# State-space stage of a decoder layer on one core: the sums over states as plain products with a standing identity, by channels, two steps behind the scan

## The chip, the cores and the metric

The kernel runs on one core of a Trainium2 chip. The metric is the device time of one execution in microseconds (us), the median of the runs shown. TensorE is called PE, VectorE DVE, ScalarE ACT, GpSimd POOL, and SyncE, which issues the transfers, SP.

## The reference, cut to what matters

A decoder layer on x of shape (16, 256, 512): a state-space block, then cross-attention, then a feed-forward block. Only the first is touched:

```python
B, L, H, DI, N, R, K = (1, 256, 512, 1024, 16, 128, 4)   # b is 16 here
hs = einsum('blh,dh->bdl', x, W_in_states); gate = einsum('blh,dh->bdl', x, W_in_gates)
hs = silu(conv(hs, conv_w) + conv_b)                     # 4 taps along l
dt = softplus((hst @ W_dt.T) @ W_dtproj.T + b_dtproj)
Bm, Cm = hst @ W_b.T, hst @ W_c.T                        # (b, l, 16)
s[l] = exp(A * dt[l]) * s[l-1] + dt[l] * Bm[l] * hs[l]   # for 1024 channels x 16 states
y[d, l] = sum_n s[l][d, n] * Cm[l, n]
y = (y + hs * D) * silu(gate)
out = einsum('bdl,od->blo', y, W_out)
```

All of it is in float32.

## The kernel before, in words

The state-space stage works through 16 batches. The 1024 channels are 8 tiles of 128 partitions, the 16 states of a tile are 4 groups of 4, and so a batch has 32 steps: step k is tile k // 4, group k % 4, four states of 256 positions. In a step

- ACT makes the decays `exp(A dt)` into PSUM, in two halves (`decays`, L708: 4 activations of 256). It waits until the bank of two steps before is free: for the product with C of step k-2, or for its scan where POOL takes the product.
- POOL makes the inputs `dt B u` (`inputs`, L830), up to four steps ahead.
- DVE runs the recurrence, in two halves (`scan`, L914). In 22 of the steps DVE also multiplies the states by C into `hc` (`times_C`, L926), two buffers that are used in turn; in the other 10, `POOL_STEPS`, the scan writes `hp` and POOL multiplies (L839), three steps behind.
- PE adds the four states and collects them over the four steps of the tile in one PSUM bank, `y_ps` (`sum_states`, L526). Each 128x128 piece of `hc` or `hp` is the stationary operand and the identity the moving one, with `is_transpose`, accumulating: the sum comes out turned, positions on the partitions, 8 products of 128 columns in a step. The skip term `u * D` starts each tile (`skip_term`, L511: 2 products with `diagD`, 128 columns each). DVE steps are summed in the step itself, POOL steps two steps later (`SUM_AT`).
- After a tile's last sum DVE multiplies by the gate (`finish_y`, L937) into `yT`. The skip term of the next tile waits for it (`y_ready`), since `y_ps` is one bank.

Besides, PE works through the products for the batches around it, called units: "s" input projection, "c" convolution (with diagonal matrices), "g" gate (made with positions on the partitions), "l" the projections to B, C and the low-rank dt, "d" dt of two tiles, "t" the turning back of two tiles of `yT` to channels, and "o" the output projection. `PRODUCTS` says how many products a unit has and `PER` how many units of the kind a batch has. `plan` deals them out over the 32 steps, so that each step has the same cost by `COST`; the order of the long ones is `LONG`, and short ones start at the steps in `SHORT`. Each unit goes to one of 3 PSUM banks in turn, and first waits until the unit three before has been taken out of its bank. ACT takes a unit out `LAG` steps after the step in which it ended (`evacuate`; DVE does so for "o", `add_residual`, L949), behind its own decays of that step.

PE's order in a step: units, then the skip term in every fourth step, then the sum. DVE's: scan, residual, product with C, and in every fourth step `finish_y`. Engines wait for each other by counting semaphores alone; the order on each engine is as written. The last batch has no "s", "c", "g", "l" for a next one, and its "o" is dealt out by `LAST_OUT`.

Of the kernel before, what the change touches and what calls it, by code (L numbers as in the profile page):

```python
# [48 lines left out]
SHORT = [(0, "d", 1, 0), (3, "t", 3, -1), (6, "d", 2, 0), (11, "t", 0, 0), (12, "d", 3, 0), (18, "t", 1, 0),  # L49
         (23, "d", 0, 1), (26, "t", 2, 0)]  # L50
# [12 lines left out]
LAG = {"s": 2, "c": 2, "g": 2, "l": 3, "d": 2, "t": 2, "o": 1}  # L63
SKIP_COST = 0.5
# [22 lines left out]
BU_OF = [(k % BUS,) for k in range(STEPS)]  # L87


def user_before(k, buffer, of):  # L90

    return next((i for i in range(k - 1, k - STEPS - 1, -1) if buffer in of[i % STEPS]))


def plan():
# [3 lines left out]
    rate = (work + DT * SKIP_COST) / STEPS  # L99

    def room(k):
        return rate * (k + 1) - (k // CPT + 1) * SKIP_COST

# [33 lines left out]
FINISH_LATE = True  # L137
# [5 lines left out]
def state_space_phase(nc, xT, x, w_in, w_bc, w_dt, w_dtproj, w_out, chan, ident, w_ffn, bc_scratch, w_scales, x1,  # L143
                      ctxt, mask, wq, wk, chan_qk, stack_d, mask_d, x1n_d):
# [5 lines left out]
    with ExitStack() as ctx:  # L150
# [28 lines left out]
        gate = sb("gate", [P, 2, SEQT, INNER])  # L179
        du = sb("du", [P, 2 * GRP, SEQ])  # L180
        y = sb("y", [P, 2, DT, SEQ])
        yT = sb("yT", [P, 2, SEQT, P])
        bc = sb("bc", [P, CPT, 2, CHUNK])
# [22 lines left out]
        mk_rows = bu[0:BATCH, 0:3].rearrange("b i c -> b (i c)").bitcast(BF16).rearrange("b (o r t) -> b o r t", o=2, r=len(PAIRS))  # L206
# [5 lines left out]
        y_ps = ps("y_ps", [P, 4, P])  # L212
# [21 lines left out]
        b_in = [sem(f"b_in{i}") for i in range(CPT)]  # L234
# [97 lines left out]

        def pool_products(b, k):

            return b * len(POOL_STEPS) + sum(i <= k for i in POOL_STEPS)
# [13 lines left out]
        def _(sp):  # L349
# [19 lines left out]
            def spread(c, side, arrived):  # L369
# [3 lines left out]
                sp.dma_start(bc[:, c, side, :], src).then_inc(arrived[c], 16)  # L373
# [21 lines left out]
            for c in range(CPT):  # L395
                spread(c, 0, b_in)
                spread(c, 1, c_in)
# [20 lines left out]
            for b in range(BATCH):  # L418
# [8 lines left out]
                if active(f):  # L427
                    for c in range(CPT):
                        sp.wait_ge(bu_done, (b + 1) * STEPS - CPT + c + 1)
                        spread(c, 0, b_in)  # L430
# [4 lines left out]
                if active(f):  # L435
                    if b == BATCH - 2:
                        load_first_rows()
                    for c in range(CPT):
                        sp.wait_ge(hc_pool, pool_products(b, max(k for k in POOL_STEPS if k % CPT == c or k == 0)))
                        sp.wait_ge(hc_dve, half_product(b, max(k for k in DVE_STEPS if k % CPT == c), HALVES - 1))  # L440
                        spread(c, 1, c_in)
# [19 lines left out]
        def _(pe):  # L461
            pe.wait_ge(params, 2 * 16)

            def unit(bank, kind, i, f, par, lo, hi):

                n, proj = PRODUCTS[kind], proj_banks[:, bank]
                if kind == "o" and is_last(f):
                    pe.wait_ge(ev["t"], seq("t", f, (hi - 1) // GRP))
                elif lo == 0:
# [8 lines left out]
                    if kind == "t":  # L478
                        pe.wait_ge(y_ready, f * DT + GRP * i + GRP)
                    if kind == "o" and i == 0:  # L480
                        pe.wait_ge(ev["t"], (f + 1) * GROUPS)
                for k in range(lo, hi):
# [3 lines left out]
                    elif kind == "g":  # L486
                        m = pe.matmul(proj[:, :], xT_sb[:, k, i % 2 * P:(i % 2 + 1) * P],  # L487
                                      win_sb[:, k, 1, i // 2 * HID:(i // 2 + 1) * HID], start=start, stop=stop)
# [10 lines left out]
                    elif kind == "t":  # L499
                        m = pe.transpose(proj[:, k * P:(k + 1) * P], yT[:, k // SEQT, k % SEQT, :], id_sb[:, :])  # L500
# [125 lines left out]
            def tail():  # L626
                pe.wait_ge(w_added, BATCH)
# [8 lines left out]
                pe.wait_ge(ev["t"], seq("t", b, GROUPS - 2))  # L636
                unit(0, "t", GROUPS - 1, b, 1, 0, PRODUCTS["t"])
# [6 lines left out]
        def _(act):  # L644
# [13 lines left out]
            def evacuate(bank, kind, i, f, par):  # L658
# [12 lines left out]
                elif kind == "g":  # L671
                    act.activation(gate[:, par, i % 2, i // 2 * HID:(i // 2 + 1) * HID], proj[:, :], ACT.Copy).then_inc(ev["g"], 1)
# [22 lines left out]
            def decays(b, k):  # L695
# [3 lines left out]
                b0, k0 = (b, k - BACK) if k >= BACK else (b - 1, k - BACK + STEPS)  # L699
                for half in range(HALVES):  # L700
                    if not (isinstance(b, int) and b == 0 and k < BACK):
                        if k0 in POOL_STEPS:
                            act.wait_ge(scan_done, half_of(b0, k0, half))
                        else:
                            act.wait_ge(hc_dve, half_product(b0, k0, half))
                    for i in range(NS // HALVES):
                        n, bank, first = half * NS // HALVES + i, bank_of_half(k, half), i * SEQ
                        a = act.activation(states[:, bank, first:first + SEQ], dt[:, t, :], ACT.Exp,  # L708
                                           scale=negA[:, t, c * NS + n:c * NS + n + 1])
# [83 lines left out]
            def tail():  # L793
                evacuate(0, "t", GROUPS - 1, BATCH - 1, 1)

            over_batches(act, front, body, tail)

        @block.gpsimd
        def _(pool):
# [20 lines left out]
            def inputs(b, k):  # L820
# [5 lines left out]
                buf, = BU_OF[k]  # L826
                before = user_before(k, buf, BU_OF)
                if not (isinstance(b, int) and b == 0 and before < 0):
                    pool.wait_ge(scan_done, half_of(b, before, HALVES - 1))
                pool.tensor_tensor(bu[:, buf, :].rearrange("p (n l) -> p n l", n=NS),  # L830
                                   du[:, t % (2 * GRP):t % (2 * GRP) + 1, :].to_broadcast([P, NS, SEQ]),
                                   bc[:, c, 0, :].rearrange("p (n l) -> p n l", n=NS), ALU.mult).then_inc(bu_done, 1)

            def times_C(b, k):
# [4 lines left out]
                pool.tensor_tensor(h, h, bc[:, k % CPT, 1, :], ALU.mult).then_inc(hc_pool, 1)  # L839
# [32 lines left out]
        def _(dve):  # L872
# [32 lines left out]
            def scan(b, k):  # L905
# [4 lines left out]
                for half in range(HALVES):  # L910
# [3 lines left out]
                    dve.tensor_tensor_scan(dst, src, bu[:, BU_OF[k][0], cols], 0.0, ALU.mult, ALU.add).then_inc(scan_done, 1)  # L914

            def times_C(b, k):
# [4 lines left out]
                for half in range(HALVES):  # L921
# [4 lines left out]
                    dve.tensor_tensor(hc[:, i % 2, cols], states[:, bank_of_half(k, half), :], bc[:, c, 1, cols], ALU.mult)\  # L926
                       .then_inc(hc_dve, 1)

            def finish_y(b, par, t):
# [30 lines left out]
            def body(b, par):  # L960
                for k in range(STEPS):
                    scan(b, k)
                    for (kind, i), (_, at) in ROWS_AT.items():
                        if is_last(b) and at == k:
                            first_rows(kind, i)
                    if not FINISH_LATE:
                        finish(b, par, k)
# [5 lines left out]
                    if FINISH_LATE:  # L973
                        finish(b, par, k)
# [1012 lines left out]
def build(nc, ins, out):  # L1987

    def dram(name, shape, dt=F32):
# [10 lines left out]
                      ins["chan"], ins["ident"], ins["w_ffn"], dram("bc_scratch", (2 * STATES, SEQ)), w_scales, x1,  # L2000
# [49 lines left out]
```

## Time and profile before

| | |
|---|---|
| median of 3 runs | 3173.97 us (3173.22 to 3177.13) |
| span of the profiled execution | 3175.0 us |
| PE busy | 2991.9 us (94%) |
| PE weight load busy | 1833.1 us (58%) |
| DVE busy | 2833.2 us (89%) |
| ACT busy | 2419.9 us (76%) |
| POOL busy | 2094.4 us (66%) |
| granted clock of PE, mean | 0.977 |

The state-space stage is the first 1750 us of the span. Busy time counts any moment in which an instruction of the engine is recorded as running. On PE an instruction's record is longer than the time until the next one may start, so the capacity that is used up is read from the distance between starts in a run of equal products.

### The profile page before, as it was taken

Reading aid. Unit: us, or ns where it says so; the run is one execution under the profiler, and the core shown is the slowest. Engines: PE = TensorE matmul, PEld = TensorE weight load, DVE = VectorE, ACT = ScalarE, POOL = GpSimd, SP = SyncE. Lnnn points to the kernel's source line nnn. Section 1 sums busy time; section 2 is a strip of 40 time slices with the busy share of each in tenths; the row PEclk is TensorE's granted clock in tenths of the full one; section 3 lists DMA queues with packets and bytes.
Section 4 is the critical chain, followed back from the end, with each engine's and each line's share of the span. In section 5 each row is a group of like instructions: output and inputs, shape, how many; then the busy total and the mean of one; then the engine's idle time right before and its main releaser. Section 6 shows DMA issues by size and latency. Waiting matters only on the chain. (4 is left out here: it accounts for less than half of the span.)

```text
span 3175.0 us, 47891 instructions
## 1 busy us (share of the span) xinstructions
PE 2991.9 (94%) x16134; PEld 1833.1 (58%) x16134; DVE 2833.2 (89%) x4149; ACT 2419.9 (76%) x4531; POOL 2094.4 (66%) x1207
## 2 busy tenths in 40 slices
PE   7899999999999999999987699999999999799998
PEld 4777677767776777777755244444444444244444
DVE  6999999999999999999998788888888888288887
ACT  4888888888888888888875177777777777577786
POOL 5999999999999999999998234334334334100000
PEclk9999999999999999999998699999999999899999
DMA  4112211222022202220221656655655653221111
GB/s 176 32 46 81 81 49 43 80 81 69 23 80 81 79 13 80 84 81 15 77 96 64 180 163 178 182 181 174 186 181 171 183 180 113 101 77 47 47 41 37
DMA packets 164389, 311.97 MB, mean 98 GB/s; under 512 B 22736, under 2 KB 80208, under 8 KB 164000
## 3 DMA queue, kind: packets, MB, share of 16 engines
q1 hardware_dynamic: 158784, 299.53, 29.6%
q10 hardware_dynamic: 5360, 9.38, 1.0%
q8 instruction: 129, 2.11, 0.3%
q14 instruction: 116, 0.95, 0.1%
HBM read 217.16 MB, written 91.69 MB: 97 GB/s over the span
## 5 line engine op out<-in xcount | busy, mean ns | idle before, releaser
L830 POOL TENSOR_TENSOR bu<-du,bc 128x1024 f32<-128x1024 f32 x512 | 1199.0, 2370 | 32.1 <-DMA bc<-bc_scratch 29.9
L708 ACT ACTIVATE states<-dt,negA 128x256 f32<-128x256 f32 x2048 | 852.8, 463 | 240.2 <-DVE hc L926 229.4
L914 DVE TENSOR_TENSOR_SCAN states<-states,bu 128x512 f32<-128x512 f32 x704 | 821.5, 1212 | 10.5 <-ACT states L708 8.2
L1568 DVE TENSOR_REDUCE mmax<-s_ps 128x1 f32<-128x512 f32 x1024 | 673.0, 686 | 126.1 <-PE s_ps L1288 105.2
L1413 ACT ACTIVATE pt<-s_ps 128x512 f32<-128x512 f32 x1024 | 579.6, 595 | 209.5 <-PE s_ps L1297 203.7
L926 DVE TENSOR_TENSOR hc<-states,bc 128x512 f32<-128x512 f32 x704 | 445.7, 674 | 1.6 <-DMA bc<-bc_scratch 1.6
L1288 PE MATMUL s_ps<-kst,qst 102*128 102x512 bf16 x1024 | 400.5, 393 | 28.6 <-DMA kst<-mask_d 19.3
L526 PEld LDWEIGHTS y_ps<-id_sb,hc 128*128 128x128 f32 x2816 | 330.7, 143 | 122.9 <-DVE hc L926 58.2
L526 PE MATMUL y_ps<-id_sb,hc 128*128 128x128 f32 x2816 | 377.1, 277 | 22.8 <-DVE hc L926 22.8
L1297 PE MATMUL s_ps<-qst,kst 105*128 105x512 bf16 x1024 | 387.4, 382 | 5.8 <-ACT pt L1413 3.9
L839 POOL TENSOR_TENSOR hp<-hp,bc 128x1024 f32<-128x1024 f32 x160 | 379.5, 2372 | 2.8 <-DVE hp L914 1.9
L914 DVE TENSOR_TENSOR_SCAN hp<-states,bu 128x512 f32<-128x512 f32 x320 | 372.2, 1204 | 5.2 <-ACT states L708 5.2
L1308 PE MATMUL pv_ps<-pt,vaug 128*32 128x512 f32 x2048 | 272.1, 604 | 1.6 <-ACT pt L1413 1.2
L1288 PEld LDWEIGHTS s_ps<-kst,qst 102*128 102x128 bf16 x1024 | 100.0, 98 | 298.6 <-DVE mmax L1568 187.3
L490 PE MATMUL proj<-xpad,diagW 128*128 128x256 f32 x960 | 245.1, 385 | 27.6 <-ACT xpad L667 27.6
L485 PE MATMUL proj<-xT_sb,win_sb 128*128 128x256 f32 x1024 | 252.8, 384 | 16.0 <-DMA win_sb<-in_w_in 7.2
L487 PE MATMUL proj<-win_sb,xT_sb 128*128 128x512 f32 x512 | 243.0, 594 | 0.0
L1817 PE MATMUL gu_ps<-gu,xqT 128*128 128x512 bf16 x1024 | 234.9, 383 | 8.0 <-ACT xqT L1870 6.3
L502 PE MATMUL proj<-wout_sb,y 128*128 128x512 f32 x512 | 240.8, 600 | 1.3 <-ACT y L679 1.3
L490 PEld LDWEIGHTS proj<-xpad,diagW 128*128 128x128 f32 x960 | 173.7, 191 | 67.8 <-issue 49.1
L485 PEld LDWEIGHTS proj<-xT_sb,win_sb 128*128 128x128 f32 x1024 | 189.1, 193 | 39.0 <-issue 10.7
L526 PE MATMUL y_ps<-id_sb,hp 128*128 128x128 f32 x1280 | 171.6, 278 | 8.2 <-POOL hp L839 7.4
(172 smaller groups left out, 4170.6 us busy)
## 6 DMA issues: line engine op xcount, KB each, us to landing
bc<-bc_scratch SPq DMA_DIRECT2D x128, 512.0 KB, 5.2
stack_d<-parts SPq DMA_DIRECT2D x180, 256.0 KB, 3.0
qst<-stack_d SPq DMA_DIRECT2D x64, 384.0 KB
kst<-stack_d SPq DMA_DIRECT2D x64, 384.0 KB
x<-xres SPq DMA_DIRECT2D x31, 512.0 KB, 4.8
w_raw<-in_w_ffn SPq DMA_DIRECT2D x48, 256.0 KB, 2.8
w_raw<-in_w_ffn SPq DMA_DIRECT2D x16, 768.0 KB, 7.3
xT_sb<-in_xT SPq DMA_DIRECT2D x16, 512.0 KB, 6.0
```

The source lines that it names most:

```text
L485: m = pe.matmul(proj[:, 0:SEQ], win_sb[:, k, 0, i * P:(i + 1) * P], xT_sb[:, k, :], start=start, stop=stop)
L490: m = pe.matmul(proj[:, 0:SEQ], diagW[:, i, k, :], xpad[:, i % 2, k:k + SEQ], start=start, stop=stop)
L526: m = pe.matmul(y_ps[:, i, :], src[:, n * SEQ + i * P:n * SEQ + (i + 1) * P], id_sb[:, :], start=False, stop=(c == CPT - 1 and n == NS - 1 ...
L708: a = act.activation(states[:, bank, first:first + SEQ], dt[:, t, :], ACT.Exp, scale=negA[:, t, c * NS + n:c * NS + n + 1])
L830: pool.tensor_tensor(bu[:, buf, :].rearrange("p (n l) -> p n l", n=NS), du[:, t % (2 * GRP):t % (2 * GRP) + 1, :].to_broadcast([P, NS, SEQ ...
L839: pool.tensor_tensor(h, h, bc[:, k % CPT, 1, :], ALU.mult).then_inc(hc_pool, 1)
L914: dve.tensor_tensor_scan(dst, src, bu[:, BU_OF[k][0], cols], 0.0, ALU.mult, ALU.add).then_inc(scan_done, 1)
L926: dve.tensor_tensor(hc[:, i % 2, cols], states[:, bank_of_half(k, half), :], bc[:, c, 1, cols], ALU.mult)\
L1288: pe.matmul(s1_ps[:, n % S_BANKS, :], qst[0:ROWS1, par, u, tt * P:(tt + 1) * P], kst[0:ROWS1, par, u, :], start=True, stop=True).then_inc( ...
L1297: pe.matmul(s2_ps[:, n % S_BANKS, :], kst[0:ROWS2, par, u, st * P:(st + 1) * P], qst[0:ROWS2, par, u, :], start=True, stop=True).then_inc( ...
L1413: act.activation(pt[:, g % 2, u % HG, st, :], s2_ps[:, score(b, u, st) % S_BANKS], ACT.Exp).then_inc(exp_done, 1)
L1568: dve.tensor_reduce(mmax[:, u // HG, c:c + 1], s1_ps[:, n % S_BANKS], AX.X, ALU.max).then_inc(s1_free, 1)
```

## The change

The sums are turned round: the identity is the stationary operand and the states are the moving one, in a plain product of 256 columns, so that the sum has channels on the partitions. The gate is made in that layout too, `finish_y` writes `y` directly, and the "t" units with their evacuations go. The sums of all steps, and the skip term with them, are made two steps later. `finish_y` moves to DVE's step k with (k - 2) % 4 == 0, ahead of the product with C. The plan drops "t", counts a skip term as 1 and a gate unit as 8 products of 256 columns; the order in `LONG` stays. Other edits rename (`bc` to `bcB` and `bcC`, `BU_OF` to `k % BUS`) or move the mask rows' scratch from `bu` to `y`.

```diff
-PRODUCTS = {"s": HK, "c": TAPS, "g": HK, "l": 2 * DT, "d": GRP, "t": GRP * SEQT, "o": DT}
-COST = {"s": 1, "c": 1, "g": 2, "l": 1, "d": 1, "t": 0.25, "o": 2}
-PER = {"s": DT, "c": DT, "g": 4, "l": 1, "d": GROUPS, "t": GROUPS, "o": SEQT}
+PRODUCTS = {"s": HK, "c": TAPS, "g": GRP * HK, "l": 2 * DT, "d": GRP, "o": DT}
+COST = {"s": 1, "c": 1, "g": 1, "l": 1, "d": 1, "o": 2}
+PER = {"s": DT, "c": DT, "g": GROUPS, "l": 1, "d": GROUPS, "o": SEQT}
...
-SHORT = [(0, "d", 1, 0), (3, "t", 3, -1), (6, "d", 2, 0), (11, "t", 0, 0), (12, "d", 3, 0), (18, "t", 1, 0),
-         (23, "d", 0, 1), (26, "t", 2, 0)]
+SHORT = [(0, "d", 1, 0), (6, "d", 2, 0), (12, "d", 3, 0), (23, "d", 0, 1)]
...
                     elif kind == "g":
-                        m = pe.matmul(proj[:, :], xT_sb[:, k, i % 2 * P:(i % 2 + 1) * P],
-                                      win_sb[:, k, 1, i // 2 * HID:(i // 2 + 1) * HID], start=start, stop=stop)
+                        t, h = GRP * i + k // HK, k % HK
+                        m = pe.matmul(proj[:, k // HK * SEQ:(k // HK + 1) * SEQ], win_sb[:, h, 1, t * P:(t + 1) * P],
+                                      xT_sb[:, h, :], start=(h == 0), stop=(h == HK - 1))
...
-                    elif kind == "t":
-                        m = pe.transpose(proj[:, k * P:(k + 1) * P], yT[:, k // SEQT, k % SEQT, :], id_sb[:, :])
...
             def skip_term(b, par, t):
 
-                if not (isinstance(b, int) and b == 0 and t == 0):
+                if b * DT + t > 0:
                     pe.wait_ge(y_ready, b * DT + t)
-                for i in range(SEQT):
-                    pe.matmul(y_ps[:, i, :], u[:, par, t, i * P:(i + 1) * P], diagD[:, t, :],
-                              start=(i == 0), stop=False, skip_group_check=True)
+                pe.matmul(y_ps[:, :], diagD[:, t, :], u[:, par, t, :], start=True, stop=False, skip_group_check=True)
...
-                    for i in range(SEQT):
-                        m = pe.matmul(y_ps[:, i, :], src[:, n * SEQ + i * P:n * SEQ + (i + 1) * P], id_sb[:, :],
-                                      start=False, stop=(c == CPT - 1 and n == NS - 1), is_transpose=True,
-                                      skip_group_check=True)
+                    m = pe.matmul(y_ps[:, :], id_sb[:, :], src[:, n * SEQ:(n + 1) * SEQ],
+                                  start=False, stop=(c == CPT - 1 and n == NS - 1), skip_group_check=True)
...
+            def tile_sums(b, par, k):
+
+                if k % CPT == 0:
+                    skip_term(b, par, k // CPT)
+                sum_states(b, k)
...
                 for k in range(STEPS):
-                    if k % CPT == 0 and k - SUM_AT in POOL_STEPS:
-                        sum_states(b, k - SUM_AT)
...
-                    if k % CPT == 0:
-                        skip_term(b, par, k // CPT)
-                    if k not in POOL_STEPS:
-                        sum_states(b, k)
-                    if k % CPT and k - SUM_AT in POOL_STEPS:
-                        sum_states(b, k - SUM_AT)
+                    if k >= SUM_AT:
+                        tile_sums(b, par, k - SUM_AT)
+                    elif b > 0:
+                        tile_sums(b - 1, 1 - par, k - SUM_AT + STEPS)
...
-                elif kind == "t":
-                    act.activation(y[:, par, GRP * i:GRP * i + GRP, :].rearrange("p t l -> p (t l)"), proj[:, :], ACT.Copy)\
-                       .then_inc(ev["t"], 1)
...
-                if not (isinstance(b, int) and b == 0 and t < 2):
-                    dve.wait_ge(mm["t"], b * GROUPS + (t - 2) // GRP + 1)
-                dve.tensor_tensor(yT[:, t % 2], gate[:, par, :, t * P:(t + 1) * P], y_ps[:, 0:SEQT, :], ALU.mult).then_inc(y_ready, 1)
+                if t == 0 and b > 1:
+                    dve.wait_ge(mm["o"], (b - 1) * PER["o"])
+                dve.tensor_tensor(y[:, par, t, :], gate[:, par, t, :], y_ps[:, :], ALU.mult).then_inc(y_ready, 1)
 
             def finish(b, par, k):
-                if k == 0 and active(b - 1):
-                    finish_y(b - 1, 1 - par, DT - 1)
-                elif k and k % CPT == 0:
-                    finish_y(b, par, k // CPT - 1)
+
+                t = (k - SUM_AT) // CPT - 1
+                if (k - SUM_AT) % CPT == 0 and t >= 0:
+                    finish_y(b, par, t)
+                elif (k - SUM_AT) % CPT == 0 and active(b - 1):
+                    finish_y(b - 1, 1 - par, t + DT)
```

## Rows read from the trace of the kernel before

**Rows 1.** The page's first part, and two rows of its 40 slices.
```profile
PE 2991.9 (94%) x16134; PEld 1833.1 (58%) x16134; DVE 2833.2 (89%) x4149; ACT 2419.9 (76%) x4531; POOL 2094.4 (66%) x1207
...
PE   7899999999999999999987699999999999799998
...
PEclk9999999999999999999998699999999999899999
```

**Rows 2.** Stretches: length, busy time and instructions by engine, clock, DMA share, GB/s.
```profile
310.00:800.00 490.00, 473.85 (x2548) 355.75 (x2547) 481.27 (x559) 413.49 (x858) 484.83 (x240) 1.00 0.20 68
```

**Rows 3.** ACT's evacuation of "l", once a batch, in order of time.
```profile
134.92 0.36 ACT L676 ACTIVATE bc_sb<-proj 32x256 f32<-32x256 f32 x1
240.41 0.36 ACT L676 ACTIVATE bc_sb<-proj 32x256 f32<-32x256 f32 x1
...
1594.65 0.36 ACT L676 ACTIVATE bc_sb<-proj 32x256 f32<-32x256 f32 x1
```

**Rows 4.** Groups by line and shape, 800 to 1012 us.
```profile
L830 POOL TENSOR_TENSOR bu<-du,bc 128x1024 f32<-128x1024 f32 x66 | 154.8, 2381 | 0.0
L708 ACT ACTIVATE states<-dt,negA 128x256 f32<-128x256 f32 x262 | 109.1, 463 | 29.2 <-DVE hc L926 28.4 <-DVE hp L914 0.5
...
L526 PE MATMUL y_ps<-id_sb,hc 128*128 128x128 f32 x360 | 46.9, 273 | 0.0
...
L490 PE MATMUL proj<-xpad,diagW 128*128 128x256 f32 x134 | 33.8, 382 | 3.2 <-ACT xpad L667 3.2
...
L526 PE MATMUL y_ps<-id_sb,hp 128*128 128x128 f32 x168 | 22.0, 274 | 0.1
...
L682 ACT ACT_TABLE_LOAD x8 | 10.3, 1283 | 1.9 <-PE proj L497 1.8
...
L511 PE MATMUL y_ps<-diagD,u 128*128 128x128 f32 x64 | 9.7, 274 | 0.0
...
L497 PE MATMUL proj<-dtlow,wdtp_sb 128*128 128x256 f32 x32 | 8.4, 386 | 3.5 <-DVE xres L949 3.5
...
L685 ACT ACTIVATE dt<-proj,chan_sb 128x256 f32<-128x256 f32 x16 | 6.7, 471 | 0.1
L937 DVE TENSOR_TENSOR yT<-gate,y_ps 128x256 f32<-128x256 f32 x16 | 6.6, 411 | 4.4 <-PE y_ps L526 3.2 <-issue 0.9
...
L667 ACT ACTIVATE xpad<-proj 128x256 f32<-128x256 f32 x16 | 5.7, 369 | 1.1 <-PE proj L485 1.0
...
L679 ACT ACTIVATE y<-proj 128x512 f32<-128x512 f32 x8 | 4.6, 581 | 0.1
...
L500 PE MATMUL proj<-id_sb,yT 128*128 128x128 f32 x32 | 4.8, 272 | 0.0
```

**Rows 5.** Matmuls in order of time, runs of equal ones merged: start, length, count.
```profile
768.83 4.46 PE L502 MATMUL proj<-wout_sb,y 128*128 128x512 f32 x10
...
821.23 0.61 PE L511 MATMUL y_ps<-diagD,u 128*128 128x128 f32 x4
821.67 1.04 PE L526 MATMUL y_ps<-id_sb,hc 128*128 128x128 f32 x8
...
822.98 1.89 PE L485 MATMUL proj<-xT_sb,win_sb 128*128 128x256 f32 x8
...
827.09 1.70 PEld L490 LDWEIGHTS proj<-xpad,diagW 128*128 128x128 f32 x8
```

**Rows 6.** DVE in order of time, around 822 us.
```profile
822.26 1.26 DVE L926 TENSOR_TENSOR hc<-states,bc 128x512 f32<-128x512 f32 x2
...
823.45 2.32 DVE L914 TENSOR_TENSOR_SCAN hp<-states,bu 128x512 f32<-128x512 f32 x2
...
825.69 2.32 DVE L914 TENSOR_TENSOR_SCAN states<-states,bu 128x512 f32<-128x512 f32 x2
```

**Rows 7.** PE in order of time, in the last batch.
```profile
1721.27 1.97 PE L526 MATMUL y_ps<-id_sb,hc 128*128 128x128 f32 x8 [2.13 <-DVE hc L926]
```

**Rows 8.** L526 alone, whole run: what PE idled for ahead of it, us and times.
```profile
  DVE hc L926: 81.0, 130
```

More of the change, by code:

```diff
@@ L86, with fixed @@
 POOL_AT, SUM_AT = 3, 2
-BU_OF = [(k % BUS,) for k in range(STEPS)]
-def user_before(k, buffer, of):
-    return next((i for i in range(k - 1, k - STEPS - 1, -1) if buffer in of[i % STEPS]))
+SKIP_COST = 1
+def fixed(k):
+    return sum(SKIP_COST * ((i - SUM_AT) % CPT == 0) for i in range(k + 1))
 def plan():
@@ L98, in plan @@
     work = sum(PRODUCTS[kind] * COST[kind] for kind, _, _ in LONG) + sum(PRODUCTS[k] * COST[k] for _, k, _, _ in SHORT)
-    rate = (work + DT * SKIP_COST) / STEPS
+    rate = (work + fixed(STEPS - 1)) / STEPS
     def room(k):
-        return rate * (k + 1) - (k // CPT + 1) * SKIP_COST
+        return rate * (k + 1) - fixed(k)
     step, spent = 0, 0
@@ L140, with state_space_phase @@
     assert GRP * CPT * (_j - 1) - 1 <= _at < GRP * CPT * _j, (_j, _at)
-def state_space_phase(nc, xT, x, w_in, w_bc, w_dt, w_dtproj, w_out, chan, ident, w_ffn, bc_scratch, w_scales, x1,
-                      ctxt, mask, wq, wk, chan_qk, stack_d, mask_d, x1n_d):
+def state_space_phase(nc, xT, x, w_in, w_bc, w_dt, w_dtproj, w_out, chan, ident, w_ffn, bc_scratch, w_scales,
+                      x1, ctxt, mask, wq, wk, chan_qk, stack_d, mask_d, x1n_d):
     with ExitStack() as ctx:
@@ L178, in state_space_phase @@
         dt = sb("dt", [P, DT, SEQ])
-        gate = sb("gate", [P, 2, SEQT, INNER])
+        gate = sb("gate", [P, 2, DT, SEQ])
         du = sb("du", [P, 2 * GRP, SEQ])
         y = sb("y", [P, 2, DT, SEQ])
-        yT = sb("yT", [P, 2, SEQT, P])
-        bc = sb("bc", [P, CPT, 2, CHUNK])
+        bcB = sb("bcB", [P, CPT, CHUNK])
+        bcC = sb("bcC", [P, CPT, CHUNK])
         bu = sb("bu", [P, BUS, CHUNK])
@@ L233, in state_space_phase @@
         xres_in = sem("xres_in")
-        b_in = [sem(f"b_in{i}") for i in range(CPT)]
+        b_in = [sem(f"b_in{c}") for c in range(CPT)]
         c_in = [sem(f"c_in{i}") for i in range(CPT)]
@@ L331, in products, with bank_before @@
             return b * len(DVE_STEPS) + sum(i <= k for i in DVE_STEPS)
+        def bank_before(b, k):
+            n = b * STEPS + k - BACK
+            return None if n < 0 else (n // STEPS, n % STEPS)
         def pool_products(b, k):
@@ L367, in load_piece, with spread, spread_B, spread_C @@
                 sp.dma_start(w_raw[:, :], src[:, i * PART:(i + 1) * PART]).then_inc(w_piece_in, 16)
-            def spread(c, side, arrived):
+            def spread(c, side, dst, arrived):
                 first = (2 * c + side) * NS
                 src = bc_scratch[first:first + NS, :].rearrange("n l -> (n l)").partition_broadcast(P)
-                sp.dma_start(bc[:, c, side, :], src).then_inc(arrived[c], 16)
+                sp.dma_start(dst, src).then_inc(arrived, 16)
+            def spread_B(c):
+                spread(c, 0, bcB[:, c, :], b_in[c])
+            def spread_C(c):
+                spread(c, 1, bcC[:, c, :], c_in[c])
             def save_bc(f):
@@ L395, in _ @@
             for c in range(CPT):
-                spread(c, 0, b_in)
-                spread(c, 1, c_in)
+                spread_B(c)
+                spread_C(c)
             sp.wait_ge(mm["g"], PER["g"])
@@ L618, in body @@
                             unit(pos % PROJ, kind, i, b + off, par if off == 0 else 1 - par, lo, hi)
-                    if k % CPT == 0:
-                        skip_term(b, par, k // CPT)
-                    if k not in POOL_STEPS:
-                        sum_states(b, k)
-                    if k % CPT and k - SUM_AT in POOL_STEPS:
-                        sum_states(b, k - SUM_AT)
+                    if k >= SUM_AT:
+                        tile_sums(b, par, k - SUM_AT)
+                    elif b > 0:
+                        tile_sums(b - 1, 1 - par, k - SUM_AT + STEPS)
             def tail():
+                for k in range(STEPS - SUM_AT, STEPS):
+                    tile_sums(BATCH - 1, 1, k)
                 pe.wait_ge(w_added, BATCH)
@@ L671, in evacuate @@
                 elif kind == "g":
-                    act.activation(gate[:, par, i % 2, i // 2 * HID:(i // 2 + 1) * HID], proj[:, :], ACT.Copy).then_inc(ev["g"], 1)
+                    act.activation(gate[:, par, GRP * i:GRP * i + GRP, :].rearrange("p t l -> p (t l)"), proj[:, :], ACT.Copy)\
+                       .then_inc(ev["g"], 1)
                 elif kind == "l":
@@ L698, in decays @@
                     act.wait_ge(du_ready, b * GROUPS + t // GRP + 1)
-                b0, k0 = (b, k - BACK) if k >= BACK else (b - 1, k - BACK + STEPS)
+                before = bank_before(b, k)
                 for half in range(HALVES):
[L701 to L705, printed above, removed]
+                    if before is not None and before[1] in POOL_STEPS:
+                        act.wait_ge(scan_done, half_of(*before, half))
+                    elif before is not None:
+                        act.wait_ge(hc_dve, half_product(*before, half))
                     for i in range(NS // HALVES):
-                        n, bank, first = half * NS // HALVES + i, bank_of_half(k, half), i * SEQ
-                        a = act.activation(states[:, bank, first:first + SEQ], dt[:, t, :], ACT.Exp,
-                                           scale=negA[:, t, c * NS + n:c * NS + n + 1])
+                        n = half * NS // HALVES + i
+                        dst = states[:, bank_of_half(k, half), i * SEQ:(i + 1) * SEQ]
+                        a = act.activation(dst, dt[:, t, :], ACT.Exp, scale=negA[:, t, c * NS + n:c * NS + n + 1])
                     a.then_inc(decay_ready, 1)
@@ L825, in inputs @@
                     pool.wait_ge(du_ready, b * GROUPS + t // GRP + 1)
[L826 to L829, printed above, removed]
+                buf = k % BUS
+                if b * STEPS + k >= BUS:
+                    pool.wait_ge(scan_done, half_of(b, k - BUS, HALVES - 1))
                 pool.tensor_tensor(bu[:, buf, :].rearrange("p (n l) -> p n l", n=NS),
                                    du[:, t % (2 * GRP):t % (2 * GRP) + 1, :].to_broadcast([P, NS, SEQ]),
-                                   bc[:, c, 0, :].rearrange("p (n l) -> p n l", n=NS), ALU.mult).then_inc(bu_done, 1)
+                                   bcB[:, c, :].rearrange("p (n l) -> p n l", n=NS), ALU.mult).then_inc(bu_done, 1)
             def times_C(b, k):
@@ L925, in times_C @@
                     dve.wait_ge(scan_done, half_of(b, k, half))
-                    dve.tensor_tensor(hc[:, i % 2, cols], states[:, bank_of_half(k, half), :], bc[:, c, 1, cols], ALU.mult)\
+                    dve.tensor_tensor(hc[:, i % 2, cols], states[:, bank_of_half(k, half), :], bcC[:, c, cols], ALU.mult)\
                        .then_inc(hc_dve, 1)
@@ L962, in body @@
                     scan(b, k)
+                    finish(b, par, k)
                     for (kind, i), (_, at) in ROWS_AT.items():
@@ L972, in body @@
                         times_C(b, k)
-                    if FINISH_LATE:
-                        finish(b, par, k)
             def tail():
```

33 lines of the change are left out of this document (12 added, 21 removed).

## Prediction

> **What bounds the kernel now.** I began with the page's busy shares and its 40 slices [rows 1]. PE is at 9 tenths or more through nearly all of the stage that the change touches, at full clock. The stretch from 310 to 800 us [rows 2] has PE busy for 473.85 of 490 us, DVE 481.27 and POOL 484.83, ACT only 413.49. So three engines look full at once. PE's figure alone says little, because its records overlap; what counts is the distance between starts.
>
> The length of a batch comes from an instruction that runs once in it [rows 3]: from 240.41 to 1594.65 us are 13 batches, (1594.65 - 240.41) / 13 = 104.2 us. The first interval, 134.92 to 240.41, is 105.5 us although batch 0 has no "o" units; the period there is set by DVE and POOL. DVE's own work: a scan pair occupies 2.24 us (825.69 - 823.45) and a pair of products with C 1.19 us (823.45 - 822.26) [rows 6]; 32 x 2.24 + 22 x 1.19 = 97.9 us, plus eight `finish_y` at about 0.35 and two residuals at about 0.6, 101.9 us.
>
> PE's work in a batch. The distance between starts is (length of a run - one instruction) / (count - 1) [rows 4, 5]: for 256 columns (1.89 - 0.385) / 7 = 0.215 us; for 512, (4.46 - 0.60) / 9 = 0.429; for a turning sum of 128, (1.04 - 0.273) / 7 = 0.110; for the skip term, 128 plain columns, (0.61 - 0.274) / 3 = 0.112. The weight load of a 256-column product is no bound: eight take 1.70 us beside 1.89 us of products.
>
> The row to see is how many instructions a product becomes [rows 4]. The two batches of that view have 2 x 4 x 4 = 32 "t" products, and L500 has x32: one each. The sums have 8 products a step, and 360 + 168 = 528 = 66 x 8 for the 66 steps that POOL's x66 counts: one each. The skip term has 2 x 8 x 2 = 32 products and L511 has x64: **two instructions each**. "d" has 2 x 4 x 2 = 16 products and L497 x32: two each. So a plain float32 product is issued twice, and one with `is_transpose` once. Per batch, in instructions: "s" 64, "c" 64, "l" 32, "d" 16 at 0.215 = 37.8 us; "g" 32 and "o" 32 at 0.429 = 27.5; sums 256 at 0.110 = 28.2; skip 32 at 0.112 = 3.6; "t" 16 at 0.110 = 1.8. Together **98.9 us of 104.2**: PE is 95% used up, and has 5.3 us of room.
>
> **The change, part by part.**
>
> *Sums.* A step had 8 turning products, 8 x 0.110 = 0.88 us. It gets 4 plain ones of 256 columns = 8 instructions at 0.215 = 1.72 us. That the identity stands still saves nothing, as the loads lie beside the products. 32 x (1.72 - 0.88) = **+26.9 us a batch**. Bounds: the product isn't in this trace, but "s" and "c" have its shape, type, accumulation and operand memories, so 0.215 is firm; below, if it were one instruction, 0.86 a step and the term -0.6.
>
> *Skip term.* 4 x 0.112 becomes 2 x 0.215: 8 x -0.02 = -0.1 us. *"t" units.* 16 instructions go: -1.8 us on PE; on ACT 4 x 0.58 = -2.3 us [rows 4], on an engine with room, worth nothing. *Gate.* 32 x 0.429 = 13.7 becomes 64 x 0.215 = 13.8 us: nothing. *`finish_y`* has the same 128x256 shape and stays at 0.41 us. Transfers are the same in number and size; the renamed buffers cost nothing, and the mask rows' scratch serves only the start.
>
> PE's work is then 98.9 + 26.9 - 0.1 - 1.8 = **123.9 us a batch**, above DVE's 101.9: PE alone sets the period.
>
> The Trainium skill bears on this in two places. Perfetto Trace Analysis, section Transposes, says to do transposes in the transpose mode rather than by a standard matmul, as they skip arithmetic; the change gives up such products for plain ones. TensorE: Matmul & The Clock Gate, section Terms, calls the mode four times faster for FP32. In this trace [rows 4, 5] it is 2 x 0.112 against 0.110 us for 128 columns, a factor of 2. By the page a plain product would cost 0.44 us, the sums 32 x 8 x 0.33 = +84 us a batch; the trace disagrees, and the rows' term stands.
>
> *Two steps behind.* The sums waited 81.0 us for `hc` over the whole run [rows 8], at most 5 us a batch, and less in the middle (no idle time ahead of their matmuls in rows 4). This wait goes; with PE the bound it is already outside the 123.9. New waits matter more. Call E(k) the end of PE's step k; a step has about 5 cost units of 0.43 us and a sum of 1.72, 3.87 us. The product with C needs its `hc` buffer back, so the third of three DVE steps in a row (k = 3, 9, 13, 19, 31) can't end before E(k) + 0.63. Steps 10 and 14 follow such a step and finish a tile: E + 0.63, scan 2.32, `finish_y` 0.41 = E + 3.4. Behind that stands PE's skip term, and all of PE's queue behind it; the plan by the new costs gives these steps 4 units, so PE is there at E + 1.72. Each loses about **1.7 us**. The other six finishes follow a step whose buffer was freed a step or more earlier: the scan is done by E + 1.3, covered by the units.
>
> *First convolution.* c0 stands first in step 2 and needs s0 out of its bank, which ACT does in its step 3. From E(31): product 0.63, scan 2.24, half the decays of step 2 0.83, then the softplus of d1 with its two table loads 1.28 + 0.94 + 1.28, decays 1.67, copy 0.37 = 9.2 us [rows 4, 6]. PE arrives after 10 units and two sums, 4.3 + 3.4 = 7.7. **1.5 us** lost; the corresponding waits now are L490's 3.2 us in two batches [rows 4]. The wait of "d" for the residual, 3.5 us in two batches, falls away: d1 now takes the bank of o0, which ended in step 26, and o1's bank goes to s1, a step later.
>
> Sum: 123.9 + 1.7 + 1.7 + 1.5 + about 1 for semaphore gaps (now 104.2 - 98.9 - 3.4 = 1.9 are unnamed) = **129.8 us, +25.6 a batch**. Bounds: no stall at all, 123.9 (+19.7); a stall of 1.7 at all eight tiles and 3 us at c0 gives about 141, against which the other six covers speak; I take 135 as the upper one.
>
> *Ends.* Batch 0 has no "o" (13.8 us less) and no sums in its first two steps (3.4 less): 23 steps at 3.88 - 3.4 + 4 of waits = 90, then 9 steps at DVE's 3.26 = 29, 119 against 105.5 with a start that is unchanged: about +12 us. The last batch has only "d" and "o", so DVE sets it; its sums there run at the lower clock level, 0.22 a piece [rows 7] ((1.97 - 0.4) / 7), and even doubled they take 3.5 us, about a DVE step. Two sums trail at the end and the "t" units with their copy are gone from it: +3.
>
> Profile's own time 3175 + 12 + 14 x 25.6 + 3 = **3548 us**. The span is within 0.1% of the median of the runs shown, 3173.97, so I don't rescale. The later stages aren't touched.
>
> **Rivals.**
> *PE bound, waits as worked out* (3500 to 3600): speaks for it that both the count and the distance are read from shapes in the same kernel. Chance 0.72.
> *PE bound, waits hidden*: if DVE and ACT run far enough ahead, 124 to 126 us: 3175 + 6 + 14 x 20.7 = 3470. 0.11.
> *PE bound, waits multiply*: evacuations hold ACT, ACT holds decays, these `finish_y`, all tiles stall; 135 us and more: 3175 + 15 + 14 x 31 = 3624 upward. 0.12.
> *The other side: the sum isn't issued twice.* If a product with the standing identity were one instruction of 0.215, PE's work would be 96.4 us, DVE and POOL would set the period at 102 to 104, and with the waits on "d" and for `hc` gone the time 3175 - 16 x 1.5 = 3150. It decides from the point where the sum step costs under 1.1 us (PE under 104). Every plain product of this kernel speaks against it. 0.03; 0.02 for no change.
>
> The range holds the three PE cases up to a period of 135: 3450 to 3620. What a measurement can tell from no change is about 0.2%. Slower by more 0.95, within 0.02, faster 0.03.
>
> **What would show it.** L526's group should have the same count, x4096 in all, with 128x256 shapes and runs of 8 in 1.89 us; L676 every 130 us; DVE and POOL busy about 80% of the stage; PE waiting at the skip term for `finish_y` twice a batch near steps 10 and 14, and at the first L490. A sum group of x2048 would mean the last rival. A DVE that is never idle would mean that I misread its room.

## The result, and the profile after

The changed kernel takes 3573.19 us (3569.74 to 3575.2), the one before 3175.38 us beside it: a ratio of **1.1254, 95% interval 1.1238 to 1.127**. The forecast was 3548 us in a range of 3450 to 3620, slower with a chance of 0.95.

The page's first part and two of its slice rows (its span is cut in 40 equal slices, a digit is the busy share in tenths), as [rows 1] for the kernel before:

```profile
PE 3369.1 (94%) x16101; PEld 2230.3 (62%) x16134; DVE 2858.7 (80%) x4149; ACT 2404.0 (67%) x4467; POOL 2095.8 (59%) x1207
...
DVE  6778778778777778777877887888888888648887
...
PEclk9999999999999999999999997999999999989999
```

DVE and POOL are busy for about as long as before (2833.2 and 2094.4 us) in a span that is 398 us longer, and DVE's slices of the stage fall from 9 to 7 and 8. Its row on the page of the kernel before:

```profile
DVE  6999999999999999999998788888888888288887
```

PE's share is 94% in both pages, so the share says nothing; PE's busy time grew by 377 us.

The same stretch as in [rows 2]:

```profile
310.00:800.00 490.00, 470.34 (x2052) 381.95 (x2051) 387.70 (x442) 321.82 (x667) 381.82 (x189) 1.00 0.14 47
```

POOL makes 189 instructions in it instead of 240: the same 490 us hold 3.75 batches (of 130.57 us, worked out below) where they held 4.70. That is why PE's busy column hardly moves (470 against 474). For one batch it is 470.34 / 3.75 = 125.3 us against 473.85 / 4.70 = 100.7, so PE's work a batch grew by about 25 us, and the batch with it.

The identity stands still, but every product still has its own weight load. From the page's groups:

```profile
L528 PE MATMUL y_ps<-hc,id_sb 128*128 128x256 f32 x2816 | 669.4, 381 | 0.0
L528 PEld LDWEIGHTS y_ps<-hc,id_sb 128*128 128x128 f32 x2816 | 538.7, 191 | 105.6 <-issue 34.9
```

The once-in-a-batch instruction (the evacuation of "l"), as [rows 3], in order of time:

```profile
155.17 0.36 ACT L680 ACTIVATE bc_sb<-proj 32x256 f32<-32x256 f32 x1
280.25 0.36 ACT L680 ACTIVATE bc_sb<-proj 32x256 f32<-32x256 f32 x1
...
1977.64 0.36 ACT L680 ACTIVATE bc_sb<-proj 32x256 f32<-32x256 f32 x1
```

The period is (1977.64 - 280.25) / 13 = **130.57 us**, where it was 104.17. Up to ACT's step 24 of batch 1, where this instruction stands, the kernel is 280.25 - 240.41 = 39.8 us late, the 13 periods add 343.2, and the last stretch of the stage, to the first instruction of the attention stage on DVE (2151.32 us, before 1751.41), adds 173.68 - 156.76 = 16.9. The stages behind give 1.5 back; together that is the 398 us.

The groups of instructions from 800 to 1064 us, as [rows 4], two batches:

```profile
L528 PE MATMUL y_ps<-hc,id_sb 128*128 128x256 f32 x355 | 84.0, 379 | 0.0
...
L922 DVE TENSOR_TENSOR hc<-states,bcC 128x512 f32<-128x512 f32 x88 | 58.0, 683 | 40.3 <-PE y_ps L528 39.4
...
L497 PE MATMUL proj<-xpad,diagW 128*128 128x256 f32 x128 | 31.7, 380 | 3.4 <-ACT xpad L670 3.4
...
L515 PE MATMUL y_ps<-u,diagD 128*128 128x256 f32 x34 | 10.7, 397 | 6.5 <-DVE y L933 6.5
```

```profile
L926 DVE TENSOR_TENSOR hc<-states,bc 128x512 f32<-128x512 f32 x90 | 56.9, 673 | 0.0
```

The last row is of the kernel before, 800 to 1012 us. DVE now waits 39.4 us for PE to free `hc`, where it waited for nothing. PE waits in two places only: 6.5 us in two batches at the skip term, 3.4 at the first convolution (`c` of tile 0).

PE in order of time around step 14 of a batch, then DVE in the same stretch:

```profile
895.72 1.89 PE L528 MATMUL y_ps<-hc,id_sb 128*128 128x256 f32 x8
897.45 1.46 PE L491 MATMUL proj<-xT_sb,win_sb 128*128 128x256 f32 x6
898.74 0.59 PE L497 MATMUL proj<-xpad,diagW 128*128 128x256 f32 x2
900.95 0.70 PE L515 MATMUL y_ps<-u,diagD 128*128 128x256 f32 x2 [1.61 <-DVE y L933]
```

```profile
896.78 0.69 DVE L922 TENSOR_TENSOR hc<-states,bcC 128x512 f32<-128x512 f32 x1 [3.97 <-PE y_ps L528]
897.65 0.69 DVE L922 TENSOR_TENSOR hc<-states,bcC 128x512 f32<-128x512 f32 x1 [0.17 <-PE y_ps L528]
898.25 2.33 DVE L910 TENSOR_TENSOR_SCAN hp<-states,bu 128x512 f32<-128x512 f32 x2
900.50 0.40 DVE L933 TENSOR_TENSOR y<-gate,y_ps 128x256 f32<-128x256 f32 x1
```

Read from the top: 8 sum instructions from 895.72, the next product starts at 897.45, that is 1.73 us for a step's sum. As PE ends the sum, DVE may fill the buffer (897.65), then scans, then finishes the tile at 900.90, and the skip term starts 0.05 us later. The row gives 1.61 us of idle time, counted from the end of the last record. By distances PE loses more: without the wait the skip term would have started at 898.74 + 2 x 0.215 = 899.17, so 1.78 us are lost, and its second instruction comes 0.32 us behind the first (0.70 - 0.38) in place of 0.215. That makes 1.88. The wait at the first convolution, in the same way:

```profile
975.85 1.89 PE L528 MATMUL y_ps<-hc,id_sb 128*128 128x256 f32 x8
979.43 1.97 PE L497 MATMUL proj<-xpad,diagW 128*128 128x256 f32 x8 [1.69 <-ACT xpad L670]
```

It would have started at 975.85 + 8 x 0.215 = 977.57, and its eight instructions take (1.97 - 0.38) - 7 x 0.215 = 0.08 us more than their distances: 1.94 us in all.

### The profile page after: what moved, and what is told of

Its sections match the earlier page's. It is cut to its first block and busy times, and to the rows that moved or that the text cites. A ratio compares the mean times of both kernels' runs of the same rounds, so it can differ in the third digit from the quotient of the medians.

```text
span 3573.4 us, 47729 instructions
## 1 busy us (share of the span) xinstructions
PE 3369.1 (94%) x16101; PEld 2230.3 (62%) x16134; DVE 2858.7 (80%) x4149; ACT 2404.0 (67%) x4467; POOL 2095.8 (59%) x1207
## 5 line engine op out<-in xcount | busy, mean ns | idle before, releaser
L709 ACT ACTIVATE states<-dt,negA 128x256 f32<-128x256 f32 x2048 | 866.6, 465 | 673.9 <-DVE hc L922 644.6
L826 POOL TENSOR_TENSOR bu<-du,bcB 128x1024 f32<-128x1024 f32 x512 | 1196.8, 2360 | 100.7 <-DVE states L910 71.3
L922 DVE TENSOR_TENSOR hc<-states,bcC 128x512 f32<-128x512 f32 x704 | 463.3, 683 | 319.3 <-PE y_ps L528 313.0
L528 PE MATMUL y_ps<-hc,id_sb 128*128 128x256 f32 x2816 | 669.4, 381 | 0.0
L528 PEld LDWEIGHTS y_ps<-hc,id_sb 128*128 128x128 f32 x2816 | 538.7, 191 | 105.6 <-issue 34.9
L835 POOL TENSOR_TENSOR hp<-hp,bcC 128x1024 f32<-128x1024 f32 x160 | 377.5, 2359 | 307.3 <-DVE hp L910 307.3
L528 PE MATMUL y_ps<-hp,id_sb 128*128 128x256 f32 x1280 | 306.8, 383 | 4.0 <-POOL hp L835 3.9
L528 PEld LDWEIGHTS y_ps<-hp,id_sb 128*128 128x128 f32 x1280 | 245.7, 192 | 46.2 <-issue 7.2
L491 PE MATMUL proj<-xT_sb,win_sb 128*128 128x256 f32 x1024 | 255.4, 387 | 14.7 <-DMA win_sb<-in_w_in 7.6
L494 PE MATMUL proj<-xT_sb,win_sb 128*128 128x256 f32 x1024 | 246.5, 380 | 0.0
L1812 PE MATMUL gu_ps<-gu,xqT 128*128 128x512 bf16 x993 | 228.0, 383 | 15.4 <-ACT xqT L1865 13.2
L491 PEld LDWEIGHTS proj<-xT_sb,win_sb 128*128 128x128 f32 x1024 | 199.2, 195 | 44.0 <-issue 10.6
```

What stands on the lines that cost most here:

```text
L491: m = pe.matmul(proj[:, 0:SEQ], win_sb[:, k, 0, i * P:(i + 1) * P], xT_sb[:, k, :], start=start, stop=stop)
L528: m = pe.matmul(y_ps[:, :], id_sb[:, :], src[:, n * SEQ:(n + 1) * SEQ], start=False, stop=(c == CPT - 1 and n == NS - 1), skip_group_check ...
L709: a = act.activation(dst, dt[:, t, :], ACT.Exp, scale=negA[:, t, c * NS + n:c * NS + n + 1])
L835: pool.tensor_tensor(h, h, bcC[:, k % CPT, :], ALU.mult).then_inc(hc_pool, 1)
L1812: mm = pe.matmul(gu_ps[:, c % 2, side, :], xqT[:, slot % 2, k, :], gu[:, c, side, k, :], start=(k == 0), stop=(k == HK - 1))
```

## The experiments

Each kernel was timed against the kernel before on the same chip.

**Plain products in the old order.** The kernel before with the transpose mode taken out:

```diff
                         m = pe.matmul(y_ps[:, i, :], src[:, n * SEQ + i * P:n * SEQ + (i + 1) * P], id_sb[:, :],
-                                      start=False, stop=(c == CPT - 1 and n == NS - 1), is_transpose=True,
+                                      start=False, stop=(c == CPT - 1 and n == NS - 1),
                                       skip_group_check=True)
```

> The kernel before, with one edit: the sums are plain products (no transpose mode), in the old order and layout, with the data stationary and 128 columns moving. Theory (a plain float32 product is issued twice, and this alone makes PE the bound): 16 instructions a step instead of 8. At the skip term's 0.112 us a piece that is 1.79 us a step, PE's work 98.9 + 32 x 0.91 = 128 us a batch, and the time 3175 + 15 x 25 to 28 = 3550 to 3600 us, about the change's 3573. Rival (the layout, the lag and the new waits cost the time, not the double issue): under 3300 us. Second rival (with data stationary, each 0.19 us weight load bounds a 128-column product): 16 x 0.19 = 3.0 us a step, +69 us a batch, above 4000 us.

Measured: 3547.16 us, ratio 1.1171 (1.1155 to 1.1188). PE in order of time, a stretch of the stage, and two evacuations of "l":

```profile
824.02 1.95 PE L526 MATMUL y_ps<-id_sb,hp 128*128 128x128 f32 x16
```

```profile
310.00:800.00 490.00, 490.00 (x3065) 408.96 (x3064) 389.73 (x448) 334.82 (x700) 394.63 (x196) 1.00 0.14 46
```

```profile
788.93 0.36 ACT L676 ACTIVATE bc_sb<-proj 32x256 f32<-32x256 f32 x1
917.67 0.36 ACT L676 ACTIVATE bc_sb<-proj 32x256 f32<-32x256 f32 x1
```

Sixteen instructions where there were eight, (1.95 - 0.27) / 15 = 0.112 us apart; the period is 128.74 us, and PE is busy for all 490 us of the stretch. The mode alone costs 24.6 us a batch and 371 us in all, nearly as much as the whole change. Neither the layout nor the lag is needed for it, and the weight loads bound nothing. The two costs don't add up simply: here PE waits for nothing in the stretch, but the "t" units stay, and a sum step is 16 x 0.112 = 1.79 us, not 1.72.

**The order alone.** The kernel before, sums still in transpose mode, all made two steps later:

```diff
+                    if k >= SUM_AT:
+                        tile_sums(b, par, k - SUM_AT)
+                    elif b > 0:
+                        tile_sums(b - 1, 1 - par, k - SUM_AT + STEPS)
```

(and the changed `finish`, t1 and t2 one step later, the entry of `LAST_OUT` at step 20 moved to 22).

> The kernel before, with the order of the change alone: all sums and skip terms two steps later, finish_y at (k - 2) % 4 == 0 ahead of the product with C, the turn-back units t1 and t2 one step later, and one output piece of the last batch two steps later; the sums stay in transpose mode. Theory: PE's work stays at 98.9 us a batch, DVE and POOL still set about 102 to 104, so 3140 to 3190 us, near the kernel before. Rival (being two steps behind brings the waits that cost the time): PE waits 3 us or more a batch at the skip term while DVE stands full, over 3230 us.

Measured: 3326.43 us, ratio 1.0475 (1.0459 to 1.049), period (1740.62 - 255.61) / 13 = 114.2 us. My theory fell: the order alone costs 150 us although PE's work is unchanged. Who waited for whom from 800 to 1030 us (us in total, times, longest), then the stretch from 310 to 800:

```profile
DVE hc L930 <- PE y_ps L526: 23.7, 13, 3.4
...
PE proj L497 <- DVE xres L955: 7.5, 2, 3.8
...
PE y_ps L511 <- DVE yT L941: 5.0, 6, 1.3
```

```profile
310.00:800.00 490.00, 445.35 (x2348) 334.34 (x2347) 440.28 (x508) 377.36 (x790) 444.06 (x221) 0.98 0.16 55
```

No engine is full: PE is busy 445 of 490 us, DVE 440, POOL 444. They take turns. DVE waits for its `hc` buffer, which PE frees two steps late, and comes late to the tile's end, for which PE waits.

**Three `hc` buffers in the changed kernel.**

```diff
-        hc = sb("hc", [P, 2, CHUNK])
+        hc = sb("hc", [P, HCS, CHUNK])                       # HCS = 3
...
-                i = DVE_STEPS.index(k)
+                i = products(b, k) - 1
...
-                        dve.wait_ge(sum_dve, half_product(b, k, half) - 2 * HALVES)
+                        dve.wait_ge(sum_dve, half_product(b, k, half) - HCS * HALVES)
```

> The changed kernel with three hc buffers instead of two. Theory (PE waits 1.6 us at the skip terms of steps 10 and 14, because the product with C of steps 9 and 13 waits for its buffer): both waits go, the period falls from 130.57 to 127.2 to 127.4, and the time by about 15 x 3.2 = 48 us, to 3520 to 3530. Rival (finish_y is late for another reason, such as the scan's own length or ACT's decays): no gain, 3565 to 3575.

Measured: 3478.96 us, ratio 1.0955 (1.0938 to 1.0971), 94 us below the changed kernel, twice what I expected. A stretch of this kernel, and evacuations of "l":

```profile
310.00:800.00 490.00, 490.00 (x2141) 399.84 (x2141) 402.20 (x462) 340.44 (x698) 407.89 (x202) 1.00 0.15 52
```

```profile
147.63 0.36 ACT L681 ACTIVATE bc_sb<-proj 32x256 f32<-32x256 f32 x1
268.19 0.36 ACT L681 ACTIVATE bc_sb<-proj 32x256 f32<-32x256 f32 x1
...
1891.61 0.36 ACT L681 ACTIVATE bc_sb<-proj 32x256 f32<-32x256 f32 x1
```

The period is (1891.61 - 268.19) / 13 = 124.88 us and PE is never idle: this is its work alone, worked out ahead as 123.9, with about 1 us of gaps. The 5.69 us of difference to 130.57 are the three waits by distances, 1.88 + 1.88 + 1.94. The wait at the first convolution went too; in my own chain it also began with a product that waited for its buffer (step 31), which I had overlooked when I wrote the expectation. The two ends of the stage gained as well (below).

**Half of the sums left out** of the changed kernel (states 0 and 2 of each group only; the output lacks the others):

```diff
-                for n in range(NS):
+                for n in range(0, NS, NS // HALVES):
```

> The changed kernel with half of the sums left out: only states 0 and 2 of each group of four are added, so y lacks the other half of its states; all waits stay. Theory (PE's work is the bound): PE's work falls by 32 x 4 x 0.215 = 27.5 to 96.4 us a batch, under DVE's 101.9, and the time goes to 3130 to 3190 us, the time of the kernel before or a little below. Rival (the waits between PE, DVE and ACT in the new order hold the period up whatever PE's work): above 3300 us.

Measured: 3296.12 us, ratio 1.0375 (1.0357 to 1.0392), period (1719.82 - 254.90) / 13 = 112.7 us. Between the two: 277 us go with 27.5 us of PE's work a batch, but the order holds the rest, as in the run of the order alone. Two of the waits from 800 to 1030 us:

```profile
DVE hc L922 <- PE y_ps L528: 19.7, 9, 4.1
...
PE y_ps L515 <- DVE y L933: 11.7, 10, 1.8
```

**One instruction a product.** The changed kernel with the sums' operands in float32r, a type of reduced precision (hc, hp and a copy of the identity are written in it, the mask's scratch moves from `hc` to `u`):

```diff
-                    m = pe.matmul(y_ps[:, :], id_sb[:, :], src[:, n * SEQ:(n + 1) * SEQ],
+                    m = pe.matmul(y_ps[:, :], id_r[:, :].bitcast(mybir.dt.float32r), src[:, n * SEQ:(n + 1) * SEQ].bitcast(mybir.dt.float32r),
```

> The changed kernel with the sums' two operands in the reduced float32 type (float32r; hc, hp and a copy of the identity are written in it, the mask's scratch moves from hc to u), two hc buffers. The sum is of reduced precision. Theory (the double issue of a plain float32 product is the cost): the group has x1408 for hc instead of x2816, the sum step costs 4 x 0.215 us or less, PE's work is 96.4 us a batch or less, and the time is that of the run with half of the sums, 3270 to 3310 us, since the waits for the two hc buffers stay. Rival (the type doesn't change the issue): 3573 us, x2816.

Measured: 3264.41 us, ratio 1.0285 (1.0271 to 1.0299), period (1687.64 - 250.40) / 13 = 110.6, 6 us under the expected range. From the page's groups, then PE in order of time, then the weight loads (PEld) in the same stretch:

```profile
L528 PE MATMUL y_ps<-hc,id_r 128*128 128x256 f32 x1408 | 314.1, 347 | 1.8 <-DVE hc L923 1.7
```

```profile
820.00 1.02 PE L507 MATMUL proj<-wout_sb,y 128*128 128x512 f32 x2
820.46 1.04 PE L528 MATMUL y_ps<-hc,id_r 128*128 128x256 f32 x4
821.34 2.74 PE L507 MATMUL proj<-wout_sb,y 128*128 128x512 f32 x6
```

```profile
820.86 0.43 PEld L528 LDWEIGHTS y_ps<-hc,id_r 128*128 128x128 f32 x3 [0.24 <-issue]
```

There are half the instructions for the same products, and each is shorter too. The length of this run can't be divided by its count, because the first record begins while the instruction before it still has its 0.43 us to go (820.00 + 0.43 = 820.43, so until 820.86). From 820.86 to 821.34 are 0.48 us for four products, 0.12 us each, and the loads of the last three are (0.43 - 0.19) / 2 = 0.12 us apart. A product of 256 columns in float32r takes 0.12 us, where one in float32 takes 2 x 0.215 = 0.43.

So the sums are 32 x 0.48 = 15.4 us a batch, not 27.5 as in the run with half of them, and PE's work is 123.9 - 55.0 + 15.4 = 84 us, not the 96.4 expected. This kernel is 32 us faster than that run, and 12 us less of PE's work a batch points that way; no run tests that by itself.

**The same with three `hc` buffers.**

> The same with three hc buffers. Theory (double issue plus the buffer's wait are the whole loss): PE at 96 us or less, DVE and POOL set about 102 to 104 us a batch, 3130 to 3170 us, at or below the kernel before. Rival (a third cause in the new order, such as evacuations behind decays, remains): above 3200 us.

Measured: 3169.47 us, ratio 0.9987 (0.9978 to 0.9996). Both causes taken out, nothing of the 398 us is left. As PE has only 84 us of work a batch here, a third cause that costs PE less than 15 us could hide in this run; but the run with three buffers in float32 leaves no room for one, since PE is never idle from 310 to 800 us there and the period is within 1 us of its counted work. A stretch of this kernel:

```profile
310.00:800.00 490.00, 426.35 (x1927) 320.86 (x1927) 478.70 (x556) 402.82 (x834) 484.73 (x241) 0.97 0.20 67
```

**The order alone with three `hc` buffers** (bc_sb in w_raw's memory to make room).

> The kernel before with all sums two steps later, as in the run of the order alone, and three hc buffers (bc_sb shares w_raw's memory to make room). Theory (what the order alone lost, 150 us, was the buffer's wait): 3140 to 3190 us. Rival (the skip term's wait for finish_y, or the banks of the units, lost it): above 3250 us.

Measured: 3174.67 us, ratio 1.0 (0.9991 to 1.0009), 152 us below the same order with two buffers. The whole price of being two steps behind was the buffer. With the buffer the lag gains nothing either: PE's products waited 22.8 us for `hc` over the kernel before and wait 0.3 us here, and the time is the same, so these waits were not on the path:

```profile
L527 PE MATMUL y_ps<-id_sb,hc 128*128 128x128 f32 x2816 | 370.1, 275 | 0.3 <-DVE hc L932 0.3
```

The runs two steps behind, by PE's work a batch and the period: with two buffers 84 and 110.6, 96.4 and 112.7, 98.9 and 114.2, 123.9 and 130.6 us; with three buffers 84 and 104.2, 98.9 and 104.2, 123.9 and 124.9.

**Three `hc` buffers in the kernel before.**

> The kernel before with three hc buffers and nothing else (bc_sb in w_raw's memory). Theory (the sums follow their products in the same step, so the buffer is free long before): no change, 3165 to 3185 us. Rival (the buffer already costs DVE something): 3130 to 3160 us.

Measured: 3174.48 us, ratio 1.0001 (0.9992 to 1.001). No change. A sum made in its own step frees the buffer in time.

**A step of POOL moved to DVE**, on the two kernels with three buffers:

```diff
-POOL_STEPS = (0, 4, 6, 10, 14, 16, 20, 22, 25, 28)
+POOL_STEPS = (0, 4, 6, 10, 14, 20, 22, 25, 28)
```

> The run with reduced-type sums and three hc buffers, and step 16 moved from POOL_STEPS to DVE (9 steps of POOL instead of 10, hp buffers by the running count). PE has room here (87% busy). Theory (POOL, busy 98.9% of the stretch, sets the last part of the period of 104.2 us): DVE's work rises by 1.2 to 103.1 us, POOL's falls by 2.3 us, the period goes to about 103.5 and the time to 3155 to 3165 us. Rival (DVE sets it): +1.2 us a batch, 3180 to 3195 us.

Measured: 3158.44 us, ratio 0.9951 (0.9938 to 0.9963), period (1584.60 - 236.88) / 13 = 103.7.

> The same step of POOL moved to DVE in the full-precision kernel with transposing sums two steps later and three hc buffers. Theory (POOL sets it, PE at 98.9 us is close): 3160 to 3175 us. Rival (DVE or PE sets it): 3180 to 3200 us.

Measured: 3189.51 us, ratio 1.0044 (1.003 to 1.0057), period (1611.88 - 242.87) / 13 = 105.3, in the range of the rival and not of the theory. The same stretch of the first and then of the second:

```profile
310.00:800.00 490.00, 423.68 (x1949) 324.23 (x1948) 488.02 (x571) 405.90 (x843) 477.09 (x237) 0.97 0.20 67
```

```profile
310.00:800.00 490.00, 471.65 (x2531) 355.70 (x2529) 481.36 (x562) 406.51 (x848) 470.73 (x234) 0.99 0.19 65
```

With PE at 84 us of work a batch, DVE fills 488 of 490 us and POOL's relief counts. With PE at 98.9 us DVE reaches 481 only, and the move costs. The two kernels differ in their layout and units too, so that PE's work is the reason is likely, not shown. The first is the fastest kernel of the study, at the price of sums in reduced precision.

## Why the prediction was right, point by point

- *A plain float32 product is issued twice; the sum step costs 1.72 us.* Right: the page's two groups of L528 have x2816 + x1280 = 4096 as forecast, a step's sum takes 1.73 us, and the mode alone makes the time 3547 us.
- *PE's work 123.9 us a batch, the bound.* Right: 124.9 with every wait gone (three buffers).
- *The factor of 2 in the trace against the four that TensorE: Matmul & The Clock Gate of the Trainium skill, section Terms, gives.* The trace's held: 0.43 us for a plain product of 256 columns, against 2 x 0.110 in transpose mode. By the four, the period would have been above 180 us, an estimate from 98.9 us and that page's factor.
- *1.7 us twice at the skip term.* Right: 1.61 us of idle time, 1.88 by distances, at steps 10 and 14 of the batch, for the cause named, the third of three DVE steps in a row waiting for its buffer. The chain had `finish_y` done at E + 3.4; in the trace it is done at 900.90, with E at 897.45.
- *1.5 us at c0.* Right: 1.7 (3.4 in two batches), 1.94 by distances, and it went with the buffer.
- *Period 129.8.* Measured 130.57. The gaps were 1.0 us, as put; the 0.8 us are in the three waits, 5.7 by distances for the 4.9 forecast. Over 13 periods they make 10 of the 25 us by which the forecast fell short.
- *The sums waited 81.0 us for `hc`, at most 5 us a batch* [rows 8]. Misread: that view adds the idle time of the weight loads (58.2) to that of the products (22.8, so 1.4 a batch). The sum of the forecast didn't use it. From the page of the kernel before:

```profile
L526 PEld LDWEIGHTS y_ps<-id_sb,hc 128*128 128x128 f32 x2816 | 330.7, 143 | 122.9 <-DVE hc L926 58.2
L526 PE MATMUL y_ps<-id_sb,hc 128*128 128x128 f32 x2816 | 377.1, 277 | 22.8 <-DVE hc L926 22.8
```

- *The ends, +12 and +3.* Mis-sized, and with a slip: 119 against 105.5 is 13.5, not 12. Up to step 24 of batch 1 the forecast is 12 + 0.75 x 25.6 = 31 us and the trace has 39.8; for the last stretch it is 0.25 x 25.6 + 3 = 9.4 against 16.9. The step that was off is "then 9 steps at DVE's 3.26", and "so DVE sets it" for the last batch: I took it that where PE has little to do DVE runs at its own pace. With two buffers and sums two steps late it doesn't, as the order alone shows (114.2 us where no engine is full). With three buffers the same two stretches are late by 268.19 - 240.41 = 27.8 and by (2057.22 - 1891.61) - 156.76 = 8.9 us, where the forecast's way with a period of 124.9 gives 12 + 0.75 x 20.7 = 27.5 and 0.25 x 20.7 + 3 = 8.2. Added up, the forecast fell short by 10 us in the periods, 8.6 and 7.5 at the ends, less the 1.5 of the stages behind: nothing large cancelled.
- *The rival on the other side.* Its condition (96.4 us of PE's work a batch) was met by the run with half of the sums, and the other type went below it with 84. They gave 3296 and 3264 us, not the 3150 that I worked out; the buffer's wait, which I had priced at 5 us a batch only for a full PE, was missing from it. With three buffers the other type gave 3169.

What holds the period at 104.2 us in four kernels (before, and the three with three buffers and 10 POOL steps that PE doesn't bound) was not taken apart further than by the last pair of runs. It is not PE's work alone, as PE has 98.9 us of it in three of them and 84 in the fourth.

## What to carry to other kernels

Count a product's instructions before its columns: in float32, moving the data through in transpose mode was one instruction where the plain product was two, and an operand that stands still saved nothing, because it was loaded anew for every product and the loads lay beside the products anyway. When a consumer is moved some steps behind its producer, ask whether its buffers must grow with it; here two buffers and a lag of two made three engines that were each 90% full take turns, and cost 150 us with no work added. Compare stretches by batch, not by busy share: where the bound engine's work and the period grow together, its share stands still. A saving on a path of equal engines can stay hidden until the next one has been relieved too: here freeing PE gave 0.1%, and 0.5% once a step had gone from POOL to DVE.

## What the runs showed of the hardware

- Plain float32 products of 128 columns ran 0.112 us apart in runs of 16, each with a new 128x128 weight load; loads did not lengthen them.
- A product in float32r was one instruction, 256 columns in 0.12 us (four in 0.48), against two instructions of 0.215 us for float32.
- The weight was loaded again for every product though the identity stood still: 2816 loads for 2816 instructions of the group, 0.19 us each beside products 0.215 us apart.
- A record of a 256-column float32 instruction was 0.38 us long and the next began after 0.215, so idle time in the rows begins 0.16 us late: three waits shown with 1.61, 1.61 and 1.69 us cost 5.7 together, which holds the slower start behind a wait too (0.32 in place of 0.215 at the skip term).
